# Preparing the weights, biases and mask of later stages inside the first expert stage

## What is computed

```python
x = x + tanh(g_xattn[i]) * attention_i(layernorm(x), ctx)
x = x + tanh(g_ffn[i])   * ffn_i(layernorm(x))
```

```python
scale = 1.0 / clip(mean(abs(w)), 1e-5)
w_q = clip(round(w * scale), -1, 1) / scale
```

## Time and profile before

| | |
|---|---|
| median of three runs | 2626.69 us (2622.69 to 2630.85) |
| span of the profiled execution | 2621.5 us, from first to last instruction |
| mean granted TensorE clock in it | 0.888 of 2.4 GHz |
| TensorE busy | 2173.2 us (83%) |
| VectorE busy | 1795.6 us (68%) |
| ScalarE busy | 1356.0 us (52%) |
| GpSimd busy | 1222.3 us (47%) |

### The profile page before, as it was taken

One profiled execution on the slowest core, in us unless ns is written; L12 is line 12 of the kernel. 1 busy time (PEld: TensorE's weight loads), 2 busy tenths in 40 slices (PEclk: granted clock), 3 DMA queues, 4 the chain that ended last, 5 costly groups with the idle time before them and its releaser, 6 DMA issues. The chain is left out here.

```text
span 2621.5 us, 77923 instructions
## 1 busy us (share of the span) xinstructions
PE 2173.2 (83%) x32227; PEld 1664.0 (63%) x32227; DVE 1795.6 (68%) x4724; ACT 1356.0 (52%) x2507; POOL 1222.3 (47%) x1731
## 2 busy tenths in 40 slices
PE   6999999999959779993654899994799858887597
PEld 5888888888837557772543677773466536666375
DVE  4777777777743378875896678876355478999454
ACT  3555555555523268873995555551122158878232
POOL 1233433344434511105775125556466666887444
PEclk9999999999979879995676899996899977878599
DMA  5112210000026311100000011112455322322263
GB/s 157 61 64 75 76 52 25 25 23 21 20 69 179 106 51 56 57 29 14 1 1 32 30 32 54 50 47 76 126 162 160 100 79 66 98 88 77 89 183 107
DMA packets 213953, 184.49 MB, mean 70 GB/s; under 512 B 33420, under 2 KB 189654, under 8 KB 213600
## 3 DMA queue, kind: packets, MB, share of 16 engines
q1 hardware_dynamic: 194144, 142.52, 18.6%
q0 software_dynamic: 19456, 36.99, 4.0%
HBM read 102.01 MB, written 72.68 MB: 67 GB/s over the span
## 5 line engine op out<-in xcount | busy, mean ns | idle before, releaser
L449 POOL DMA_INDIRECT slots<-row,put x256 | 257.6, 1006 | 184.1 <-issue 96.1
L1797 PE MATMUL experts_H<-experts_xs_t,experts_w 128*128 128x512 f32 x576 | 266.8, 607 | 7.0 <-DMA experts_b<-in_F_b 2.7
L975 ACT ACTIVATE l_prob_t<-l_Z 128x512 f32<-128x512 f32 x256 | 132.2, 603 | 145.9 <-PE l_Z L1098 114.1
L1339 POOL TENSOR_TENSOR l_var_eps<-l_mv,eps 128x1 f32<-128x1 f32 x64 | 12.1, 189 | 407.4 <-DVE l_mv L1420 407.4
L1815 PE MATMUL experts_Y<-experts_w,experts_hid 128*128 128x128 f32 x1664 | 197.8, 275 | 3.5 <-DVE experts_y L1750 2.6
L1669 POOL DMA_INDIRECT rows<-experts_y,experts_idx x160 | 155.4, 971 | 92.8 <-DVE experts_y L1746 52.3
L1815 PEld LDWEIGHTS experts_Y<-experts_w,experts_hid 128*128 128x128 f32 x1664 | 191.7, 192 | 5.4 <-issue 5.4
L1375 DVE TENSOR_REDUCE l_top<-l_S 128x16 f32<-128x1024 f32 x64 | 78.3, 1223 | 165.6 <-PE l_S L1518 165.6
L895 DVE TENSOR_REDUCE l_top<-l_X 128x32 f32<-128x2048 f32 x64 | 146.5, 2290 | 65.1 <-PE l_X L1107 49.0
L1797 PEld LDWEIGHTS experts_H<-experts_xs_t,experts_w 128*128 128x128 f32 x576 | 106.6, 195 | 116.2 <-issue 107.5
L767 POOL TENSOR_TENSOR l_var_eps<-l_mv,eps 128x2 f32<-128x2 f32 x96 | 19.8, 207 | 332.3 <-DVE l_mv L865 232.7
(11 more groups left out here) (326 smaller groups left out, 5989.0 us busy)
## 6 DMA issues: line engine op xcount, KB each, us to landing
experts_w<-in_F_w SPq DMA_DIRECT2D x104, 256.0 KB, 2.8
l_ctx_t<-in_ctx_t SPq DMA_DIRECT2D x96, 128.0 KB, 2.3
l_q_m<-l_q_t SPq DMA_DIRECT2D x384, 32.0 KB, 1.8
experts_xs<-slots SPq DMA_DIRECT2D x40, 264.0 KB, 3.0
slots<-l_empty SPq DMA_DIRECT2D x16, 536.0 KB, 3.4
experts_xs<-slots SPq DMA_DIRECT2D x16, 536.0 KB, 4.2
slots<-l_empty SPq DMA_DIRECT2D x16, 520.0 KB
experts_xs<-slots SPq DMA_DIRECT2D x16, 520.0 KB, 4.4
```

Of the source, the lines that this page charges most:

```text
L449: pool.indirect_dma_start(self.slots, bass.IndirectOffsetOnAxis(ap=g.put[c][:, tile:tile + 1], axis=0), g.row[:, tile, self.sent_cols], No ...
L975: nc.scalar.activation(prob_t[:, t.par(PROB), r, :], Z[:, r, :], ACT.Exp).then_inc(prob_done, 1)
L1797: nc.tensor.matmul(H[:, c, :], w1_s[:, t.par(2), c, :], xs_t[:, t.par(2), :], start=True, stop=True).then_inc(h_filled[c], 1)
```

## The change

A class Early holds what three attentions and the bit-linear stage need: weights, scaled and masked biases, bias rows, minus ones, quantised weights with their scales, the mask's numbers, and one q_m for all attentions. Its tensors stay in SBUF from the start (the mask's numbers and q_m from behind attention_wide). experts0 is called with it, and behind each step t of its SP, VectorE and TensorE programs a method of Early is called that issues what is planned for that t; GpSimd sets q_m to zero once, ahead of its first step. The stages that follow lose their loads, prepare shrinks to memsets, the last of them (recip) signals ready, and the router's load moves to step 4.

The core of the diff:

```diff
+    QUANT_LOAD, MASK_LOAD, BIAS_LOAD, WEIGHT_LOAD = 3, 4, (5, 6, 7), (8, 9, 10)
+    SUM, TOTAL, SCALE, QUANT = 6, 7, 8, (9, 10)
+    HIDES = (7, 8, 9, 10)
+    WIDEN, FILL, ROWS = (8, 9, 13), (9, 10, 14), (11, 12, 15)
...
+    def landed(self, sp):
+        sp.wait_ge(self.weights_in, 16 * 9)
+        sp.wait_ge(self.quant_in, 16 * 4)
+
+    def gpsimd(self, pool):
+        self.nc.gpsimd.memset(self.q_m[:, :, :, :], 0.0).then_inc(self.cleared, 1)
+
+    def tensor(self, pe, t):
+        nc, g = self.nc, self.g
+        if t == self.TOTAL:
+            pe.wait_ge(self.w_summed, 1)
+            nc.tensor.matmul(self.bank[:, 0:2], g.const[:, C_ONES:C_ONES + P], self.w_sum[:, :], start=True, stop=True).then_inc(self.w_totalled, 1)
+        for n in (0, 2):
+            if t == self.FILL[n]:
+                out = self.bank[0:3, P * (1 + n // 2):P * (2 + n // 2)]
+                pe.wait_ge(self.widened[n], 1)
+                nc.tensor.matmul(out, self.bv_three[n][:, :], self.wo[n][:, :], start=True, stop=False)
+                nc.tensor.matmul(out, g.const[0:1, C_ONES:C_ONES + 3], self.bo[n][:, :], start=False, stop=True).then_inc(self.bias_filled[n], 1)
...
+        if t == self.SUM:
+            V.memset(self.minus_ones[:, :], -1.0)
+            dve.wait_ge(self.quant_in, 64)
+            for n in range(2):
+                last = V.tensor_reduce(self.w_sum[:, n:n + 1], self.w_raw[n][:, :], AX.X, ALU.add, apply_absolute_value=True)
+            last.then_inc(self.w_summed, 1)
+        if t in self.HIDES:
+            k = self.HIDES.index(t)
+            if k == 0:
+                dve.wait_ge(self.mask_in, 32)
+            h, part = k // 2, slice(32 * (k % 2), 32 * (k % 2) + 32)
+            V.tensor_scalar(self.hide[:, h, part, :], self.mask_raw[:, h, part, :], self.HIDE, -self.HIDE, ALU.mult, ALU.add)
...
+        for n in range(2):
+            if t == self.QUANT[n]:
+                then(V.tensor_scalar(self.w_round[:, :], self.w_raw[n][:, :], self.w_inv[:, n:n + 1], None, ALU.mult))
+                then(V.tensor_scalar(self.w_round[:, :], self.w_round[:, :], MAGIC, -MAGIC, ALU.add, ALU.add))
+                then(V.tensor_scalar(self.w_q[n][:, :], self.w_round[:, :], 1.0, -1.0, ALU.min, ALU.max))
...
@@ attention_split
-                    sp.wait_ge(cleared, 1)
...
-            for t in range(2, ITEMS + STREAM + 1):
+            for t in range(ITEMS + STREAM + 1):
+                if tail and t == 4:
+                    tail.load(sp)
                 step(Step(sp, ITEMS, t))
...
-            def clear():
-
-                nc.gpsimd.memset(q_m[:, :, :, :], 0.0).then_inc(cleared, 1)
...
-                dve.wait_ge(weights_in, LOADED)
-                V.tensor_scalar(bq_scaled[:, :], bq_s[:, :], SCALE, None, ALU.mult)
...
+                V.memset(recip[:, :, :], 1.0).then_inc(ready, 1)
@@ experts
+            def both(t):
+                step(t)
+                if early:
+                    early.vector(dve, t.t)
+
             dve.wait_ge(go, 1)
-            pipeline(dve, ITEMS, DEPTH, step)
+            pipeline(dve, ITEMS, DEPTH, both)
@@ bitlinear_ffn
-            V.memset(root[:, :, :], 1.0)
-            dve.wait_ge(weights_in, 64)
...
+            V.memset(root[:, :, :], 1.0).then_inc(ready, 1)
             dve.wait_ge(ready, 1)
```

More of the change, by code:

```diff
@@ L608, in beats, with attention_split @@
     return max(0, min(t - first + 1, n))
-def attention_split(nc, g, name, gate_col, wq, bq, wk, bk, wv, bv, wo, bo, kind, mask=None, head=None, stream=None, router=None, weights=None, out=None):
+def attention_split(nc, g, name, gate_col, kind, head=None, stream=None, router=None, weights=None, out=None):
     ITEMS = TILES // 2
     SCALE = float(1.0 / np.sqrt(np.float32(8)))
-    HIDE = float(2.0 ** 100)
     folded, stable = kind == "masked", kind == "stable"
@@ L654, in attention_split @@
         ctx_out_t = None if folded else ph.sb("ctx_out_t", [P, 2, 2, 2, 64])
-        if mask is not None:
-            mask_raw = ph.sb("mask_raw", [P, 2, TILES, 64], U8)
-            hide = ph.sb("hide", [P, 2, TILES, 64], BF16)
         X, Z = ph.ps("X", [P, 4, 512]), ph.ps("Z", [P, 4, 512])
@@ L1562, in _, with experts @@
             pipeline(pe, ITEMS, DEPTH + 5, step, UNROLL)
-def experts(nc, g, name, slots, rows, w1, b1, w2, b2, kind, gate_col, last=False):
+def experts(nc, g, name, slots, rows, w1, b1, w2, b2, kind, gate_col, last=False, early=None):
     dynamic, gated = kind == "silu", kind == "relu"
@@ L1657, in step @@
                             w2_in[t.par(2)], 16)
-            pipeline(sp, ITEMS, DEPTH, step)
+            def both(t):
+                step(t)
+                if early:
+                    early.sync(sp, t.t)
+            pipeline(sp, ITEMS, DEPTH, both)
+            if early:
+                early.landed(sp)
         @block.gpsimd
@@ L1941, in _ @@
             V.memset(mv[:, :, :, :], 1.0)
-            V.memset(root[:, :, :], 1.0)
-            dve.wait_ge(weights_in, 64)
-            for n in range(2):
-                last = V.tensor_reduce(w_sum[:, n:n + 1], w_raw[n][:, :], AX.X, ALU.add, apply_absolute_value=True)
-            last.then_inc(w_summed, 1)
-            dve.wait_ge(w_totalled, 1)
-            for k in range(2):
-                last = V.tensor_scalar(w_scale[:, :, k], W[:, 0:2], 1.0 / (D * FF), 1e-5, ALU.mult, ALU.max)
-            then(last)
-            then(V.reciprocal(w_inv[:, :], w_scale[:, :, 0]))
-            for n in range(2):
-                then(V.tensor_scalar(w_round[:, :], w_raw[n][:, :], w_inv[:, n:n + 1], None, ALU.mult))
-                then(V.tensor_scalar(w_round[:, :], w_round[:, :], MAGIC, -MAGIC, ALU.add, ALU.add))
-                then(V.tensor_scalar(w_q[n][:, :], w_round[:, :], 1.0, -1.0, ALU.min, ALU.max))
-            then(V.tensor_scalar(w_scale[:, 1, :], w_scale[:, 1, :], g.gate[:, gate_col:gate_col + 1], None, ALU.mult))
-            V.tensor_scalar(b2_s[:, :], b2_s[:, :], g.gate[:, gate_col:gate_col + 1], None, ALU.mult).then_inc(ready, 1)
+            V.memset(root[:, :, :], 1.0).then_inc(ready, 1)
             dve.wait_ge(ready, 1)
```

234 lines of the change are left out of this document (130 added, 104 removed).

## The result

The changed kernel takes 2589.47 us in the median (2583.16 to 2595.27, four runs), the kernel before 2628.77 beside it (2622.69 to 2634.59): 39.3 us less. The ratio, taken over the single runs, is 0.9868 with a 95% interval of 0.9848 to 0.9888, or 34.7 us less. Timed again in five rounds it gave 2584.62 against 2626.22 us, 41.6 us less, and by the ratio of 0.9848 (0.9822 to 0.9874) 39.9 us. One run of the kernel before took 4243.83 us in that series and counts in neither the ratio nor its interval. Two executions of the changed kernel were profiled, with spans of 2589.7 and 2581.9 us.

What follows compares the result with a forecast made beforehand. Each full stage was taken as bound, TensorE in l2, with set-up delaying only its opening. Opening gains of 36.6 us less 2.1 cost gave 34.5, so 2626.69 becomes 2592 us, range 2583 to 2605.

Steps and rivals of the forecast that it cites:

- The openings: Starts of bit-linear, l1, l2 and l3: first work begins earlier by 10.8, 7.6, 11.5 and 6.7 us, 36.6 in all.
- the sure part of l3's gain: l3's opening: the chain of combine, statistics and reciprocal root surely loses the 3.5 us memset, lower bound of the 6.7.
- the 3.0 us: l1's and l2's openings: GpSimd's q_m memset stretches the first two normalisations to about 3.58 us from 0.60.
- The new matmuls: First experts, TensorE: two bias rows of two products each and one total cost 1.4 us, 2.9 at low clock.
- VectorE's work: First experts: 20 us of new work, only the part over 3.1 us slack per step stalls, costing 0.5 us.
- GpSimd's memset: Start of the first experts: q_m's memset beside the first L1722 and L1734 costs 0 to 0.5 us, taken as 0.2.
- From sum to time: Whole kernel: gains 36.6 less cost 2.1 give 34.5 us; the median lies 5.2 above the profiled span, so 2592.
- The signs: First experts: wrong if steps 9 to 15 take 8 us or more; no step over 7.7 except with new matmuls.
- rival 1: First experts: VectorE's mask and rounding instructions hold GpSimd's scatters, adding 7.5 us, giving 2600 us; chance 0.10.
- rival 2: Openings of l1, l2, l3: another gate is late next, two thirds of gains kept, 8.6 us lost, 2601; chance 0.14.
- rival 3: TensorE, mainly l2: shifted starts make it work at 1.2 GHz instead of 2.4; 53 us so moved gives 2634; chance 0.03.
- rival 4: Openings: ready signals come no earlier because something else holds their instruction; only the cost is left, 2629 us; chance 0.02.

Runs made afterwards that it cites:

- the three kernels above: Changed kernel with l1's and l3's VectorE memsets ahead of the first item (2585.92 us), that plus late bias matmuls (2584.88), or q_m's memset back in l1, l2, l3 (2598.51).

## Why the prediction held, term by term

- **The openings**: forecast 10.8, 7.6, 11.5 and 6.7 us, measured 10.82, 7.73, 11.47 and 6.69. That each could be taken from the distance between two rows held, because nothing else stood close behind; the bit-linear stage, undone alone, gave 11.19 back.
- **Inside them** one step was wrong without harm: the memset of q_m was put down as the sure part of l3's gain and its lower bound. Put back behind the prepared opening, it was no part of the first projection's time there and cost 2.0 us in the items behind. In the kernel before it reached the bias chain by one copy, 0.8 us longer by it. So l3's gain is the bias chain's. In l1 and l2 the 3.0 us were right (2.98 and 2.98). Of l1's 7.73 us 2.98 are thus the memset and, by subtraction, 4.75 the bias chain; the early loads of weights by themselves are worth nothing. In l2 the mask has 2.03 + 3.41 = 5.4 us by the rows.
- **The new matmuls**: 1.4 forecast, 0.81 + 0.81 + 0.22 = 1.84 measured. A pair of products had been counted at 0.58; it puts 0.62 ahead of H (842.25 - 841.63), and another 0.1 to 0.2 go to what it displaces.
- **VectorE's work**: 0.5 forecast, nothing measured. The slack is 3.38 us and not 3.1: the forecast counted from the end of ScalarE's last read, but reads that start late run back to back, four in 2.42 us, and so catch up 0.28 us of the pace that TensorE's products had set them. The largest delay is 3.31, so the schedule fits by 0.07 us; the forecast of 3.2 us a bias row was close.
- **GpSimd's memset** at the start: 0.2 forecast, nothing measured (first H at 6.14 against 6.13, and 6.18 without it).
- **What was not forecast**: the first distance between items, 6.28 before and 6.50 to 7.96 in the kernels with the change. It follows the moment of the clock's rise, which differs by 2 us between two profiles of the changed kernel; between 0.2 and 1.7 us, why the rise came earliest in the profile of before is open.
- **From sum to time**: 36.7 - 1.8 = 34.9 us, inside the intervals of both measured differences (34.7 and 39.9 us by the ratios, some 5 and 7 us wide to each side). The forecast added 5.2 us as the distance of the median from the profiled span; in the changed kernel's two series it was -0.2 and 2.7 us. Each run that is listed with its own span takes 1.8 us more than it; the rest of that term is the luck of which run was profiled, and with 31.8 us between the two first spans and 39.6 to the second it is the largest uncertainty of all.
- **The signs**: the prediction called itself wrong "if steps 9 to 15 there take 8 us or more", and two of them take 8.16. That sign was badly set and not the sum: a pair of products at its own 0.58 us on a step of 7.44 already makes 8.02. The first distance of 7.88 us also passes the 7.7 that it allowed, for the reason above. The others held or nearly: first projections 2.43 and 1.76 us behind the first transposes in l1 and l2; 0.8 us more from first to last projection in l1 in one profile and 0.2 less in the other; the low clock 29.4 and 14.8 us long behind l1's first statistics against 29.7, and 14.7 and 14.5 behind l2's against 24.8.
- **The rivals**: scatters are held by back-to-back instructions of VectorE from SBUF to SBUF (1.67 to 2.22 us), but that reaches no step, so rival 1 costs nothing. A next gate (rival 2) is absent from the changed openings and appears in l3 once 2.8 us more are taken from its opening. The clock (rival 3) moves l2 between 418 and 426 us in kernels that share its opening, and l3 between 367 and 371; the nine runs of the changed kernel reach from 2576.09 us at a granted clock of 0.901 to 2595.27 at 0.887, 0.4% either way. No kernel's openings pushed it to the slower side beyond that, save perhaps l3's in the three kernels above. The ready signals came earlier (rival 4).

## What to carry to other kernels

Here set-up that stood between a barrier and a stage's first item cost its whole length, could be read off as the distance of two rows, and added up over the stages; moved under a stage whose bound is another engine it was free up to a slack that useless instructions measured, except for what it put on the bounding engine itself (1.84 us). Separate the chain from its loads before moving both: here the loads of weights were hidden anyway, and the memset, the bias chain and the mask were the gain. An opening can be shortened only until the rate of the next producer shows (4.6 us per item in l3), and a single profile is no better than TensorE's clock, here some 10 us of 2600 either way.

## What was not expected of the hardware

- A scatter of GpSimd beside back-to-back instructions of VectorE from SBUF to SBUF took up to 2.22 us instead of 0.97, beside copies from PSUM 0.97 to 0.98. The other way round, an instruction of 128x8 numbers on VectorE took 3.52 us beside a conversion of 5.70 us on GpSimd.
- TensorE kept at 2.4 GHz by useless work up to the opening fell to 1.2 GHz right behind it and stayed there for 24 us.
- Stretches with the same instructions swing in length with the clock between executions: 770.4 to 775.1 us for the first stage, 294.7 to 299.1 from first to last projection in l3. In one kernel the low clock behind l1's first statistics lasted 29.4 us in one profile and 14.8 in the other.
